# Attention's SP queue and GpSimd's bias step reordered, and unread products on TensorE in the dense stage

## What is computed

```
h = layernorm(x) * (1 + ca) + sa
x = x + ga * attn(h)          # attn: 16 heads of width 8, causal, low-rank Q, K, V and output,
                              # then layernorm and a GELU MLP 128 -> 512 -> 128 (low rank)
h = layernorm(x) * (1 + cb) + sb
x = x + gb * ffn(h)           # ffn: RMS norm; shared MLP 128 -> 512 -> 128 with ReLU;
                              # router over 8 experts, top 2 of sigmoid scores; each expert 128 -> 512 -> 128
```

## Time and profile before

| what | value |
|---|---|
| median of 3 runs | 699.83 us (698.48 to 700.15) |
| the profiled execution: its own time | 706.22 us |
| the profiled execution: span from first to last instruction | 704.5 us |
| busy: PE, PEld, DVE, ACT, POOL | 607.5, 401.2, 450.2, 408.1, 301.2 us |
| mean granted TensorE clock | 0.959 of 2.4 GHz |
| transfers | 100.40 MB, mean 143 GB/s |

### The profile page before, as it was taken

How to read it: one execution, slowest core, us unless ns; L and a number is a source line. 1 busy time by engine, 2 the same in 40 slices (tenths; PEclk the granted TensorE clock), 3 DMA queues, 4 the chain that set the end, 5 groups by cost and what they waited for, 6 DMA issues and landing times.

```text
span 704.5 us, 16609 instructions
## 1 busy us (share of the span) xinstructions
PE 607.5 (86%) x5841; PEld 401.2 (57%) x5841; DVE 450.2 (64%) x1346; ACT 408.1 (58%) x718; POOL 301.2 (43%) x478
## 2 busy tenths in 40 slices
PE   3988888887888879778868977999897999999997
PEld 2643444443444434334324666766765999999993
DVE  5759888888899857767732878777673222222227
ACT  0432678687677758656658465676434555555550
POOL 4232334253443605232313438666671445545452
PEclk9999799999999989998989988999899999999999
DMA  9653142443343424340463411211236788878779
GB/s 196 196 168 87 57 131 101 141 140 111 120 154 121 148 84 153 118 133 28 146 178 112 131 44 55 81 51 49 66 94 189 216 226 222 240 224 226 230 217 316
DMA packets 85842, 100.40 MB, mean 143 GB/s; under 512 B 13808, under 2 KB 67736, under 8 KB 85664
## 3 DMA queue, kind: packets, MB, share of 16 engines
q1 hardware_dynamic: 76608, 86.53, 41.1%
q0 software_dynamic: 4544, 9.45, 3.7%
q10 hardware_dynamic: 4608, 3.35, 1.9%
HBM read 59.89 MB, written 37.31 MB: 138 GB/s over the span
## 4 chain that ended last, share of the span: by engine, by line
PE 46%; DMA 13%; DVE 12%; SPq 9%; issue 9%; ACT 6%; POOL 5%; POOLq 0%; ACTq 0%; DVEq 0%
PE ps_r L1543 7%; PE ps_s L1533 7%; PE ps_pv L1351 6%; DVE row_max L1735 6%; PE ps_pv L1429 4%; DMA arena<-slots_d 3%; PE ps_r L1289 3%; POOL slots_d L931 3%; PE ps_r L1294 3%; DMA k_d<-arena_early 2%; DMA arena<-y_d 2%; PE ps_s L1334 2%; SPq L612 2%; PE ps_s L1437 2%; SPq L609 2%
## 5 line engine op out<-in xcount | busy, mean ns | idle before, releaser
L1735 DVE TENSOR_REDUCE row_max<-ps_r 128x1 f32<-128x384 f32 (+3 forms) x384 | 211.4, 594 | 45.8 <-PE ps_r L1294 43.1
L1007 ACT ACTIVATE arena<-ps_s 128x1024 f32<-128x1024 f32 (+1 forms) x192 | 168.6, 882 | 86.8 <-PE ps_s L1334 85.1
L977 POOL DMA_INDIRECT y_d<-arena,target x78 | 74.9, 960 | 86.5 <-DVE arena L1942 74.3
L1351 PE MATMUL ps_pv<-arena 128*32 128x512 f32 (+3 forms) x1024 | 95.4, 471 | 0.0
L1289 PEld LDWEIGHTS ps_r<-ident_h,later_q 64*128 64x128 bf16 x768 | 24.7, 94 | 121.3 <-DVE row_max L1735 78.9
L1289 PE MATMUL ps_r<-ident_h,later_q 64*128 64x64 bf16 (+1 forms) x768 | 49.5, 206 | 42.7 <-DVE row_max L1735 42.3
L1938 DVE TENSOR_TENSOR arena<-ps_r,arena_early 128x256 f32<-128x256 f32 x39 | 16.6, 425 | 108.2 <-PE ps_r L1543 108.2
L931 POOL DMA_INDIRECT slots_d<-arena,slots x64 | 65.3, 1020 | 18.2 <-issue 18.2
L1294 PE MATMUL ps_r<-arena 48*128 48x384 bf16 (+3 forms) x512 | 70.8, 310 | 0.0
L1334 PE MATMUL ps_s<-arena 51*128 51x256 bf16 (+3 forms) x512 | 70.6, 310 | 0.0
L1543 PEld LDWEIGHTS ps_r<-arena 128*128 128x128 f32 x480 | 58.2, 192 | 1.5
(11 more groups left out here) (240 smaller groups left out, 1129.0 us busy)
## 6 DMA issues: line engine op xcount, KB each, us to landing
arena<-in_ew SPq DMA_DIRECT2D x30, 514.0 KB
ctx_d<-ctx_raw SPq DMA_DIRECT2D x32, 256.0 KB, 2.6
arena<-q_d SPq DMA_DIRECT2D x64, 96.0 KB, 2.7
arena<-k_d SPq DMA_DIRECT2D x64, 96.0 KB, 2.7
arena<-slots_d SPq DMA_DIRECT2D x39, 132.0 KB, 3.0
arena_early<-in_ew SPq DMA_DIRECT2D x9, 514.0 KB, 3.8
arena<-y_d SPq DMA_DIRECT2D x8, 512.0 KB, 6.8
q_d<-arena_early SPq DMA_DIRECT2D x8, 384.0 KB, 2.5
```

The source lines that it names most:

```text
L977: pool.indirect_dma_start(y_d[:], bass.IndirectOffsetOnAxis(ap=target[:, k, c:c + 1], axis=0), res[:, k, c, :], None).then_inc(put[k], 16)
L1007: act.activation(dst, src, ACT.Exp, scale=SCALE).then_inc(exp_done, 1)
L1351: mm = pe.matmul(ps_pv[32 * j:32 * j + 32, kt * P:S], v_sb[b % 2][:, kt, GROUPS * j + g, :], probs[:, p % 2, at:at + length], start=(kt == ...
L1735: dve.reduce_max(row_max[:, m % 2, js[0] % 2, j:j + len(js), i], src, AXIS.X).then_inc(max_taken, 1)
```

## The change

On SP, in attention: a step now begins with the store of the context; the sums are loaded next (`load_sums`); the loads of `rec_rows` and of the context (`ctx_t`) both move to the step after, 4b+7 (`load_rec_and_ctx`), in this order; the store of the maxima follows, then the store of the reciprocal, the K store, the loads of the stacks, now one group a step in four successive steps, the load of the maxima, and the Q store last. On VectorE the reciprocal moves from behind unit 10 to behind unit 5. On GpSimd `out_bias` is added a step earlier, in step 4b+2.

On TensorE, in the dense stage: `keep_busy(count, into)` issues `count` products of the identity with `w_fc1` (512 columns, f32) into a PSUM bank that nobody reads before it is written again. Two stand before `router` in iterations 2 to 4 (with the wait on `summed` moved ahead of them), two at the head of iterations 8 to 10 (ahead of `counts` and `transpose_n3`, behind a wait on `n3t_out`), two before `l2` in iterations 11 and 12, and two before `turn(0)`: 18 products.

```diff
-NORM_EARLY = 3
+NORM_EARLY, BIAS_AT = 3, 2
...
-                    def load_ctx(b):
+                    def load_sums(b):
 
                         for k in range(2):
                             wait(sp, ctx_stored[k], 32 * (b + 1))
                         wait(sp, rec_ready, b)
+                        sums_d = ctx_d[b % 2].rearrange("(j r) g s -> r j g s", j=JH)[DH].rearrange("j g s -> j (g s)")
+                        sp.dma_start(sums[:], sums_d.rearrange("j (c s) -> j c s", s=HEADS * S // P)).then_inc(sum_loaded, 16)
+
+                    def store_rec(b):
+
+                        wait(sp, rec_ready, b + 1)
+                        wait(sp, rec_loaded, 16 * b)
+                        sp.dma_start(rec_d.rearrange("h (c s) -> (h c) s", s=HEADS * S // P), recs[:]).then_inc(rec_stored, 16)
+
+                    def load_rec_and_ctx(b):
+
+                        wait(sp, ctx_ready, b)
+                        wait(sp, rec_stored, 16 * (b + 1))
+                        sp.dma_start(rec_rows[:], rec_d.unsqueeze(1).to_broadcast([HEADS, DH, S])).then_inc(rec_loaded, 16)
                         cells = ctx_d[b % 2].rearrange("(j r) g s -> r j g s", j=JH)
-                        sp.dma_start(sums[:], ...)
-                        wait(sp, ctx_ready, b)
                         for j in range(JH):
                             sp.dma_start(ctx_t[...], ...)
-                    def move_rec(b):
...
                     def step(n):
-                        for g, later in ((0, 0), (1, 0), (2, 1), (3, 2)):
-                            b = batch_at(n, LOAD_AT + later)
-                            if b is not None:
-                                load_stack(b, g, "k" if b == 0 and g == 0 else "qk")
+                        if 0 <= n - 2 < NG:
+                            store_ctx(n - 2)
                         if batch_at(n, CTX_AT) is not None:
-                            load_ctx(batch_at(n, CTX_AT))
+                            load_sums(batch_at(n, CTX_AT))
+                        if batch_at(n, CTX_AT + 1) is not None:
+                            load_rec_and_ctx(batch_at(n, CTX_AT + 1))
                         if 0 <= n + LAG - 1 < NG:
                             store_max(n + LAG - 1)
-                        if batch_at(n, K_OUT_AT - 1) is not None:
-                            store_stack(batch_at(n, K_OUT_AT - 1), 0)
+                        if batch_at(n, CTX_AT) is not None:
+                            store_rec(batch_at(n, CTX_AT))
                         if batch_at(n, K_OUT_AT) is not None:
                             store_stack(batch_at(n, K_OUT_AT), 1)
...
-                        if 0 <= n - 2 < NG:
-                            store_ctx(n - 2)
+                        for g in range(GROUPS):
+                            b = batch_at(n, LOAD_AT + g)
+                            if b is not None:
+                                load_stack(b, g, "k" if b == 0 and g == 0 else "qk")
                         if 0 <= n + LAG - 1 < NG:
                             load_max(n + LAG - 1)
-                        if batch_at(n, CTX_AT) is not None:
-                            move_rec(batch_at(n, CTX_AT))
+                        if batch_at(n, K_OUT_AT - 1) is not None:
+                            store_stack(batch_at(n, K_OUT_AT - 1), 0)
...
-                        b = batch_at(n, 3)
+                        b = batch_at(n, BIAS_AT)
...
+                    def keep_busy(count, into):
+
+                        for k in range(count):
+                            pe.matmul(into, ident[:], w_fc1[:], start=True, stop=True)
+
                     for n in range(0, B + L2_LAG):
+                        if n >= B and n < B + 3:
+                            pe.wait_ge(n3t_out, n - 2)
+                            keep_busy(2, ps_s1[:, 0, :])
                         if real(n - 3):
                             counts(n - 3)
                         if real(n):
                             fc1(n)
                         if real(n - 2):
                             transpose_n3(n - 2)
+                        if n in (2, 3, 4):
+                            pe.wait_ge(summed, n)
+                            keep_busy(2, ps_pv[:])
+                        if n >= B + 3:
+                            keep_busy(2, ps_s1[:, 0, :])
                         if real(n - L2_LAG):
                             l2(n - L2_LAG, 0)
...
                         if n - L2_LAG == B - 1:
+                            keep_busy(2, ps_s1[:, 0, :])
                             turn(0)
...
-                            if u == 10 and batch_at(n, CTX_AT) is not None:
+                            if u == 5 and batch_at(n, CTX_AT) is not None:
```

More of the change, by code:

```diff
@@ L644, in load_ctx @@
                         wait(sp, rec_ready, b)
+                        sums_d = ctx_d[b % 2].rearrange("(j r) g s -> r j g s", j=JH)[DH].rearrange("j g s -> j (g s)")
[8 more added lines that the diff above has]
+                        sp.dma_start(rec_rows[:], rec_d.unsqueeze(1).to_broadcast([HEADS, DH, S])).then_inc(rec_loaded, 16)
                         cells = ctx_d[b % 2].rearrange("(j r) g s -> r j g s", j=JH)
-                        sp.dma_start(sums[:], cells[DH].rearrange("j g s -> j (g s)").rearrange("j (c s) -> j c s", s=HEADS * S // P)).then_inc(sum_loaded, 16)
-                        wait(sp, ctx_ready, b)
                         for j in range(JH):
```

## The result

Over 20 executions each, the changed kernel has a median of 709.4 us and the kernel before 701.8 us. The ratio is 1.0101, with a 95% interval of 1.0075 to 1.0127. (A ratio leaves out executions that took over 1.5% longer than their kernel's fastest; here one of 877 us and the profiled one of the changed kernel are among them.) The forecast was 689.0 us, with a range that ended at 698.5. The profiled execution took 713.3 us (span 711.5), against 706.2 (span 704.5).

A forecast was written before the change was run, and what follows sets the result against it. No single engine was taken as the bound; the engines feed each other closely. -13.0 - 1.1 + 0.3 = -13.8 us gave 692.4 from the profiled 706.2, or 686.0 from the median 699.8; the middle is 689, range 682.5 to 698.5.

The forecast's parts named there:

- -13.0 and -0.8: Forecast totals: attention -16.0 + 3.0 = -13.0 us; dense stage -1.1 and +0.3 us.
- I take 0.6 us, five times ... 3.0 us back, bounds 0.5 to 5.5: Attention, reciprocal at unit 5: VectorE waits 0.6 us for the sums in batches 0 to 4, 3.0 us lost.
- Attention: -16.0: Attention steps: removing the sums' wait and GpSimd's lateness gains 16.0 us, measured against undisturbed steps.
- batch 3's 5.8 us: Attention, batch 3's step 4b+7: falls from 15.26 us to the undisturbed 9.43, gaining 5.8 us.
- The step of 9.43 us: Attention: length of an undisturbed step 4b+7, the standard for the gains of batches 1 and 3.
- GpSimd: Attention: with L900 gone from behind `ctx_n`, the split can start 3.7 us sooner; TensorE's longest wait was 2.33 us.
- Batch 7, "about 1.0 us is lost": Batch 7: context loads behind `rec_rows` start `ctx_n` 2.61 us later; about 1.0 us lost, bounds 0 and 2.6.
- Dense stage, -1.1 and +0.3: Unread products: -1.1 us net in iterations 2 to 4; +0.3 from iteration 8 to `turn(0)`, bounds -1.3 and +2.5.
- The first: Rival, attention: the sums come 2.5 us late rather than 0.6, 9.5 us more, 698.5 us; chance 0.13.
- The second: Rival, attention: context loads behind `rec_rows` delay `ctx_n`, splits 1.4 us later in seven batches; 706 us; chance 0.09.
- the 11.9 at the sums: Attention: gain at the sums, 11.9 less 3.0 us, set against the losses in the slower rival of chance 0.09.
- lose the clock elsewhere: Attention, sign against the prediction: steps stay at 9.4 us in the sum but lose the clock elsewhere; no size given.

The follow-up runs named there:

- dense part alone: The kernel before with only the unread keep_busy products added: 701.0 us, ratio 0.9967 to the kernel before.
- attention part alone: The changed kernel with all keep_busy calls left out: 709.7 us, ratio 1.0134 to the kernel before.
- the hold-up at unit 5: Changed kernel, reciprocal back at unit 10, plus two unread maxima on VectorE at unit 5 of each step 4b+6: ratio 1.0079 to the kernel before.
- the repeated run: Second measurement of the changed kernel with only the reciprocal moved back to unit 10: 697.7 us, ratio 0.9944 to the kernel before.
- the first experiment: The changed kernel with only the reciprocal moved back from unit 5 to unit 10: 696.5 us, ratio 0.9959 to the kernel before.

## Why the prediction was wrong

Against the profiled execution of before, the changed kernel lost 4.7 us to the dense stage's memset, 0.9 from there to `turn(2)`, and 1.4 in the expert stage. The forecast had -13.0 and -0.8.

By the ratios, the forecast was -10.8 us to the median of 699.83 and the measured change is +7.1 (1.0101), 18 us apart. Some 7 of them are the first bullet: with the reciprocal back at unit 10 the kernel gains about 10 us, where the forecast had put 3.0. The other 10 or so are in the kernel with unit 10 too (0.9959 and 0.9944, a gain of 3 to 4 us where the forecast without that term has 13.8); they are the third and the fifth bullet.

The start of the memset that opens the dense stage shows how much of this one trace can tell. Traces with the same attention code differ by up to 5.5 us:

| attention code | memset starts at, us |
|---|---|
| before (and dense part alone) | 384.2, 379.4 |
| biases earlier (and with products) | 378.1, 372.6 |
| new order, unit 10 (five traces; in two of them batch 7's loads early) | 370.9 to 373.6 |
| new order, unit 5: the change (and attention part alone) | 388.9, 384.3 |
| the same with the sums first | 369.3 |
| unit 7, sums first, batch 7's loads early | 368.7 |
| unit 10 with the hold-up at unit 5 | 381.9 |
| old order, unit 5 | 406.7 |

- **The step that failed: "I take 0.6 us, five times ... 3.0 us back, bounds 0.5 to 5.5".** The event was forecast closely: in batch 2 the sums were to be issued 3.6 us sooner in the step and to be waited for 0.1 to 1.1 us; they were issued at 211.36, where the whole step lies 2.5 us later, and waited for 0.55. But the wait was priced at its own length. I had just read from the earlier trace rows that stalls of 2 to 4 us cost their length plus the clock behind them, and didn't ask it of a new, shorter one. Measured with everything else equal, the early reciprocal costs 1.4% by the ratios (1.6% against the repeated run), 10 to 11 us; by the traces it is 10.7 to 18.1 us up to the memset. Of the one or the other 7.3 are waits. What the runs show in the place of the 3.0 us is a stall of TensorE that in four or five of six batches cost it the high clock for about 6.8 us. All upper bounds of this term assumed a landing time; none assumed another price.
- **The size of the waits was low as well:** 7.3 us in six batches, not 3.0. Batches 0 and 4 had 2.34 and 2.08.
- **"Attention: -16.0" came out where no wait took its place:** 13.4 us in the first experiment's trace, with 5.4 us of waits for the maxima in it. This is the second step that failed, for it was measured from one execution with large stalls (706.2 us, against medians of 702 to 705 in three of the four series), and the forecast took half of that excess as untouched. By the medians the first experiment gained 6.8 and 4.3 us, by the ratios 3 to 4. Most of the sixteen wasn't there to be had in a typical execution: batch 3's 5.8 us were absent in the dense part's trace, and SP's order, which was to remove the waits for the sums, is worth nothing that can be told apart (0.9899 with the old one, 0.9873 and 0.9886 with the new). The step of 9.43 us that was taken for undisturbed was a little long as well, 9.07 to 9.08 in the first experiment.
- **GpSimd:** right in the main. L900 is gone from behind `ctx_n`; alone this is worth about 5 us. It halves the waits for the split maxima (3.5 to 1.7 us). That there are none in the changed kernel is due to the early reciprocal, which lets `ctx_n` start sooner: with unit 10 they are 5.4 us, and with unit 7 none.
- **Batch 7, "about 1.0 us is lost":** right place, too small. The context's loads start 2.6 us later, and then take longer to land, beside the dense stage's own transfers. `ctx_n` came 4.2 us later in the changed kernel, above the bound of 2.6, and the edit that puts it right is worth some 3.3 us.
- **Dense stage, -1.1 and +0.3:** within what was measured (0.9967, 0.9923 to 1.0011). The `fc2` of iterations 2 and 3 ran in 3.82 us as forecast; that of iteration 4 lost the clock in the changed kernel, behind an idle time of 2.12 us that the pair of 1.88 left in front of the router, and kept it in the run of the dense part alone, with 2.13:

```profile
435.85 1.88 PE L1506 MATMUL ps_pv<-w_fc,ident 128*128 128x512 f32 x4
439.84 1.21 PE L1475 MATMUL ps_r<-arena_early,arena 128*128 128x8 f32 x8 [2.12 <-DVE slots L1876]
440.91 5.26 PE L1434 MATMUL ps_pv<-w_fc,arena 128*128 128x128 f32 x32
```

- **The rivals.** The first (the wait for the sums moves rather than goes) had the right place, and ended at no change because it too counted only length. The second, the one on the slower side, had the wrong mechanism: against the start of step 4b+8, `ctx_n` came sooner in batches 0 to 4 and 1.8 us later in batch 5, and TensorE waited for no split. Its sum has slips as well: 7 x 1.4 is 9.8 and not 9.5, and the 11.9 at the sums stands on no row. The last sentence of the prediction, steps that "lose the clock elsewhere", named what happened, without a price or a chance.

## What to carry to other kernels

A wait is to be priced with what the engine behind it loses afterwards: here half a microsecond on VectorE cost 2.8 in one execution, because TensorE stood idle and its clock halved for 6.8 us, and 0.4 in another, where the clock held. Before work is moved to an earlier place in a tightly coupled list, ask whether its data are there then; a reciprocal two units later, its load half a microsecond sooner and batch 7's loads early turned 1% slower into 2% faster. And a gain measured from one profiled execution is a gain over that execution.

## What the runs showed of the hardware that was not expected

At unit 5, TensorE's idle time was 0.5 us more than VectorE's wait. In the traces of the changed kernel, its attention part and the run with the sums first, nine idle times of 1.45 to 2.84 us were each followed by a fall of the clock; of the nine from 1.08 to 1.28 us (with the hold-up run's), five were; of the five from 0.71 to 1.00 us, none. At other places it isn't so clear-cut. Batch 0 of the run with unit 7 fell after 0.81 us, and with the reciprocal at unit 10 batch 0's clock fell in some traces (the kernel before, the repeated first experiment) and not in others (the first experiment), each with 0.52 and 0.65 us as the only idle times over 0.3 us there. Also at unit 10, idle times of 2.19 us (batch 4 of the kernel before) and 2.52 us (the dense part alone) left that step's clock at 1.00, and the step was longer by little more than the idle time (10.92 and 11.35 us against 8.48), while those of 2.56 and 3.46 us (batches 1 and 3 of the kernel before) came with a fall.
